# A product-key expert lookup: forming and searching 136 of each head's 256 pair sums

## What is computed

```python
sim = jnp.einsum('pbnhd,hkpd->pbnhk', queries, keys)
v0, i0 = jax.lax.top_k(sim[0], TOPK)
all_scores = v0[..., :, None] + i0[..., None, :].astype(v0.dtype)
all_scores = all_scores.reshape(*all_scores.shape[:-2], -1)
scores, pk_indices = jax.lax.top_k(all_scores, TOPK)
h = jax.nn.gelu(jnp.einsum('bnd,bnhkd->bnhk', q, jnp.take(weight_down_embed, pk_indices, axis=0)))
h = h * jax.nn.softmax(scores, axis=-1)
out = jnp.einsum('bnhk,bnhkd->bnd', h, jnp.take(weight_up_embed, pk_indices, axis=0))
```

## Time and profile before

| | us |
|---|---|
| median of 3 runs | 2607.98 |
| lowest and highest run | 2607.81, 2615.81 |
| the profiled execution | 2608.87 |
| its span, first to last instruction | 2607.1 |

### The profile page before, as it was taken

How to read it: one execution, slowest core, us unless ns; L and a number is a source line. 1 busy time by engine, 2 the same in 40 slices (tenths; PEclk the granted TensorE clock), 3 DMA queues, 4 the chain that set the end, 5 groups by cost and what they waited for, 6 DMA issues and landing times.

```text
span 2607.1 us, 30788 instructions
## 1 busy us (share of the span) xinstructions
PE 2241.5 (86%) x11214; PEld 1274.1 (49%) x11214; DVE 1378.6 (53%) x4080; ACT 725.1 (28%) x1573; POOL 813.7 (31%) x532
## 2 busy tenths in 40 slices
PE   1999984998967999988899999988999989888863
PEld 0455552443323444446654567668666633444431
DVE  5455676778965666651142443420222232599996
ACT  3111121221004444432211365552111110244442
POOL 2028888887875556640000000000000000022221
PEclk9998776997988999999999989998999989989977
DMA  9982222222227666642000020003000050000000
GB/s 358 419 322 3 3 3 19 4 4 19 3 35 203 162 169 174 170 119 110 1 11 38 9 98 1 1 1 131 1 1 1 1 133 0 1 4 9 8 8 12
DMA packets 90264, 180.59 MB, mean 69 GB/s; under 512 B 65109, under 2 KB 66070, under 8 KB 74135
## 3 DMA queue, kind: packets, MB, share of 16 engines
q1 hardware_dynamic: 44367, 176.77, 20.9%
q0 software_dynamic: 45072, 1.46, 5.1%
q10 hardware_dynamic: 674, 0.39, 0.1%
HBM read 110.27 MB, written 68.31 MB: 68 GB/s over the span
## 4 chain that ended last, share of the span: by engine, by line
PE 45%; POOL 19%; DVE 14%; issue 7%; DMA 5%; SPq 5%; ACT 4%; DVEq 0%; ACTq 0%; POOLq 0%
POOL edge_table L503 16%; PE banks L189 10%; PE banks L1999 6%; PE banks L2026 5%; DMA edge_table<-arena 5%; SPq L293 5%; PE banks L1432 3%; PE banks L1255 3%; PE banks L1268 2%; PE banks L1810 2%; PE banks L1837 2%; PE banks L1824 2%; POOL arena L1212 2%; PE banks L1859 2%; DVE arena L1180 1%
## 5 line engine op out<-in xcount | busy, mean ns | idle before, releaser
L189 PE MATMUL banks<-arena 128*125 128x512 f32 (+1 forms) x1280 | 601.7, 619 | 84.3 <-ACT arena L2503 75.0
L503 POOL DMA_INDIRECT edge_table<-arena x313 | 490.8, 1568 | 248.1 <-DMA edge_table<-arena 157.7
L189 PEld LDWEIGHTS banks<-arena 128*125 128x125 f32 x1280 | 245.2, 200 | 374.6 <-issue 278.8
L1180 DVE TENSOR_TENSOR arena<-banks,arena 125x500 f32<-125x500 f32 x200 | 208.4, 1051 | 148.9 <-ACT banks L1232 146.5
L1212 POOL TENSOR_TENSOR arena<-arena 125x500 f32<-125x500 f32 x180 | 222.8, 1248 | 147.0 <-DVE arena L1180 141.5
L1255 PE MATMUL banks<-arena 64*125 64x250 f32 x800 | 141.3, 430 | 50.9 <-DVE arena L1180 44.4
L2337 POOL MEMSET arena<- 128x1024 f32 x2 | 1.8, 952 | 579.8 <-DVEq L140 579.8
L1947 DVE SCALAR_TENSOR_TENSOR arena<-banks,arena 125x512 f32<-125x512 f32 x80 | 60.1, 751 | 203.7 <-PE banks L2026 203.7
L1232 ACT ACTIVATE banks<-banks 125x500 f32<-125x500 f32 x200 | 114.5, 573 | 169.7 <-PE banks L1258 169.3
L183 PE MATMUL banks<-arena 125*128 125x125 f32 x560 | 94.8, 309 | 69.5 <-DVE arena L177 50.0
L1999 PEld LDWEIGHTS banks<-arena 128*128 128x128 f32 x1280 | 144.2, 192 | 6.9 <-issue 6.8
(11 more groups left out here) (318 smaller groups left out, 3598.7 us busy)
## 6 DMA issues: line engine op xcount, KB each, us to landing
edge_table<-arena SPq DMA_DIRECT2D x24, 2250.0 KB, 36.1
arena<-edge_table SPq DMA_DIRECT2D x50, 984.4 KB
arena<-L_ffn_W SPq DMA_DIRECT2D x4, 2048.0 KB, 8.2
arena<-edge_table SPq DMA_DIRECT2D x50, 114.3 KB
adjacency<-arena SPq DMA_DIRECT2D x50, 109.4 KB
arena<-adjacency SPq DMA_DIRECT2D x10, 546.9 KB
edge_table<-arena POOLq DMA_INDIRECT x313, 3.0
arena<-x SPq DMA_DIRECT2D x1, 2240.0 KB
```

What stands on the lines that cost most here:

```text
L189: last = nc.tensor.matmul(dst, xT[:, i, :], w[:, i, 0:n], start=(i == 0), stop=(i == k - 1))
L503: pool.indirect_dma_start(d["table"], bass.IndirectOffsetOnAxis(ap=cell[0:EP, c:c + 1].bitcast(U32), axis=0), vals[0:EP, c * ROW:(c + 1) * ...
L1180: nc.vector.tensor_tensor(P_g[n % PRING][0:TP, :].rearrange("p (e n) -> p e n", e=2), two_scores(n), ring[(c * TILES + b) % RING][0:TP, :, ...
```

## The change

A head's table is no longer formed whole. The values `v0` come sorted, so row a of the table belongs to the a-th largest value. The first 8 rows are formed with all 16 columns, 128 cells; of the other 8 rows only the cell in the column with the largest key index is formed, 8 cells. A cell in one of these rows and another column is beaten by at least 16 others, so the 16 largest are among the 136. (`PAIR_CELLS` is 136, `LOW` 128.)

- VectorE, after the cast: the largest index of each head (`fmax_p`, a reduction), and at the start of `pairs` a comparison of each index with it, which gives 1 in its column and 0 elsewhere (`largest_p`).
- GpSimd: two additions in place of one (8 x 128 and 8 x 8 cells), the second after the reduction; the product of `S` and `M` over 1088 cells; and a new product `U` that spreads the 8 cells of each head back over their 128 places by the comparison. `U` has one buffer and waits for TensorE's sums of the tile before.
- VectorE's four search groups and ScalarE's two groups run over 136 columns of a head in place of 256. Their counts stay.
- TensorE sums the heads in two groups: 8 products of 128 columns from `S` into the first half of the bank, and 8 of 128 columns from `U` into the second.

```diff
@@ -2337,19 +2342,33 @@
                 last = nc.gpsimd.memset(w, 0.0)
             last.then_inc(s_zeroed, 1)
             for t in range(TILES):
-                pool.wait_ge(p_f, t + 1)
+                pool.wait_ge(p_f, 3 * t + 1)
                 if t >= 2:
                     pool.wait_ge(p_ws, t - 1)
                 S, M = S_p[t % 2][0:TP, :], M_p[t % 2][0:TP, :]
+                by_cell = S.rearrange("p (h n) -> p h n", h=HEADS)
+                v0 = v0_p[t % 2][0:TP, :].rearrange("p (h a) -> p h a", a=TOPK)
+                f0 = f0_p[t % 2][0:TP, :].rearrange("p (h b) -> p h b", b=TOPK)
+                fmax = fmax_p[t % 2][0:TP, :].unsqueeze(2)
+                is_max = largest_p[t % 2][0:TP, :].rearrange("p (h b) -> p h b", b=TOPK)
                 nc.gpsimd.tensor_tensor(
-                    S.rearrange("p (h a b) -> p h a b", h=HEADS, a=TOPK),
-                    v0_p[t % 2][0:TP, :].rearrange("p (h a) -> p h a", a=TOPK).unsqueeze(3)
-                    .to_broadcast([TP, HEADS, TOPK, TOPK]),
-                    f0_p[t % 2][0:TP, :].rearrange("p (h b) -> p h b", b=TOPK).unsqueeze(2)
-                    .to_broadcast([TP, HEADS, TOPK, TOPK]), ALU.add).then_inc(p_sp, 1)
+                    by_cell[:, :, 0:LOW].rearrange("p h (a b) -> p h a b", a=TOP_ROWS),
+                    v0[:, :, 0:TOP_ROWS].unsqueeze(3).to_broadcast([TP, HEADS, TOP_ROWS, TOPK]),
+                    f0.unsqueeze(2).to_broadcast([TP, HEADS, TOP_ROWS, TOPK]), ALU.add).then_inc(p_sp, 1)
+                pool.wait_ge(p_f, 3 * t + 2)
+                nc.gpsimd.tensor_tensor(by_cell[:, :, LOW:PAIR_CELLS], v0[:, :, TOP_ROWS:TOPK],
+                                        fmax.to_broadcast([TP, HEADS, TOPK - TOP_ROWS]), ALU.add).then_inc(p_sp, 1)
 
                 pool.wait_ge(p_e, 2 * t + 2)
                 nc.gpsimd.tensor_tensor(S, S, M, ALU.mult).then_inc(p_w, 1)
+                pool.wait_ge(p_w, 2 * t + 1)
+                pool.wait_ge(p_f, 3 * t + 3)
+                if t >= 1:
+                    pool.wait_ge(p_ws, t)
+                nc.gpsimd.tensor_tensor(
+                    U_p[0:TP, :].rearrange("p (h a b) -> p h a b", h=HEADS, b=TOPK),
+                    by_cell[:, :, LOW:PAIR_CELLS].unsqueeze(3).to_broadcast([TP, HEADS, TOPK - TOP_ROWS, TOPK]),
+                    is_max.unsqueeze(2).to_broadcast([TP, HEADS, TOPK - TOP_ROWS, TOPK]), ALU.mult).then_inc(p_w, 1)
...
                 nc.vector.tensor_copy(f0_p[t % 2][0:TP, :], i0_p[t % 2][0:TP, :].bitcast(U32)).then_inc(p_f, 1)
+                dve.wait_ge(p_f, 3 * t + 1)
+                nc.vector.tensor_reduce(fmax_p[t % 2][0:TP, :], by_head(f0_p[t % 2], TOPK), AX_X, ALU.max).then_inc(p_f, 1)
 
             def pairs(t):
 
                 S, M, top = S_p[t % 2], M_p[t % 2], top_p[t % 2]
-                dve.wait_ge(p_sp, t + 1)
+                dve.wait_ge(p_f, 3 * t + 2)
+                nc.vector.tensor_tensor(by_head(largest_p[t % 2], TOPK), by_head(f0_p[t % 2], TOPK),
+                                        fmax_p[t % 2][0:TP, :].unsqueeze(2).to_broadcast([TP, HEADS, TOPK]),
+                                        ALU.is_equal).then_inc(p_f, 1)
+                dve.wait_ge(p_sp, 2 * t + 2)
...
@@ -2571,12 +2599,17 @@
 
             def weights(t):
 
-                pe.wait_ge(p_w, t + 1)
+                pe.wait_ge(p_w, 2 * t + 1)
                 if t >= 1:
                     pe.wait_ge(p_x, t)
                 for h in range(HEADS):
-                    last = nc.tensor.matmul(bank(3)[0:TP, 0:KEYS], ident[0:TP, 0:TP],
-                                            S_p[t % 2][0:TP, KEYS * h:KEYS * (h + 1)],
+                    nc.tensor.matmul(bank(3)[0:TP, 0:LOW], ident[0:TP, 0:TP],
+                                     S_p[t % 2][0:TP, PAIR_CELLS * h:PAIR_CELLS * h + LOW],
+                                     start=(h == 0), stop=(h == HEADS - 1))
+                pe.wait_ge(p_w, 2 * t + 2)
+                for h in range(HEADS):
+                    last = nc.tensor.matmul(bank(3)[0:TP, LOW:KEYS], ident[0:TP, 0:TP],
+                                            U_p[0:TP, (KEYS - LOW) * h:(KEYS - LOW) * (h + 1)],
                                             start=(h == 0), stop=(h == HEADS - 1))
                 last.then_inc(p_ws, 1)
```

25 lines of the change are left out of this document (16 added, 9 removed).

## The result

The changed kernel takes 2565.48 us (median; 2562.40 to 2571.48), the kernel before 2609.51 beside it (2607.81 to 2615.81). The ratio is 0.982, 95% interval 0.9804 to 0.9836. The forecast was 2556 in a range of 2546 to 2570: the time is in the range and 9.5 us above the forecast. The profiled execution took 2563.54 us, with a span of 2561.7.

A forecast was written before the change was run, and what follows sets the result against it. VectorE's own work plus one wait per tile for GpSimd's pair sums bounds the kernel. Savings of 40.7 + 9.8 + 1.3 = 51.8 us gave 2557.1 for a profile and 2556 us for the median, range 2546 to 2570.

The forecast's parts named there:

- Searches: VectorE's 32 searches a tile, first search to first exponential: 256 to 136 columns, 12.66 to 8.59 us; ten tiles 40.7 us.
- Pair sums: From the cast's start to the first search: 4.00 to 3.07 us in tiles 2 to 7; 9.8 us in all.
- ScalarE and GpSimd hidden: ScalarE's exponentials and relus end 1.6 us earlier; GpSimd's products stay hidden by 6 us before the next pair sums.
- The comparison: VectorE's added instruction before the first search: +0.2 us, able to meet GpSimd's addition in tiles 8 and 9 only.
- TensorE: Its loop per tile takes 27.4 us against a 28.6 us period: hidden by 1.2 us, output projection near 2.0 us.
- The tail and the clock: After tile 9's first exponential starts: ScalarE 1.6 us earlier, the split sum costs 0.3; 1.3 us gained.
- The sum against a median: 51.8 us off a profiled 2608.87 us, 0.9 above the median: 2557.1 for a profile, 2556 for the median.
- (a): TensorE becomes the bound, its clock staying lower from output projection through queries: loop 30.9 us, time 2568; chance 0.08.
- (b): VectorE's searches do not shorten with length: only 11 us gained, time 2597; chance 0.05.
- (c): VectorE's searches shorten in full proportion to length: time 2542; chance 0.04.
- (d): GpSimd's two additions end over 8.0 us after the cast's start, making the kernel slower; at 9 us, 2621; chance 0.03.
- (e): The change does not do what it says, only possible by a longer search of another kind; given no chance of its own.

The follow-up runs named there:

- the searches alone: Kernel before with all 256 sums formed but VectorE's four search groups run over 136 columns of a head: 2576.55 us, ratio 0.9848.
- the comparison elsewhere: Changed kernel with the comparison taken off VectorE, GpSimd subtracting the largest index and ScalarE making the mark: 2566.73 us, ratio 0.9806.
- The sums alone: Kernel before with the new pair sums, reduction and comparison, but searches, exponentials, relus and product still over 256 columns: 2605.61 us, ratio 0.9963.
- the first trace: First profile of the changed kernel against the kernel before: 2565.48 us, ratio 0.9820, last stage 297.6 us.
- the second: Changed kernel profiled once more, nothing altered: 2570.36 us, ratio 0.9825 to the kernel before, last stage 301.1 us.
- the repeated half: Changed kernel with the second half of TensorE's head sum formed twice (2567.15 us, ratio 0.9818) or three times (2585.04 us, ratio 0.9884).
- four lengths: Kernel before searching 200 or 72 columns (2595.93 and 2551.02 us, one run each), beside 136 and 256; a search took 0.353, 0.220, 0.286, 0.412 us.

## Why the prediction was right, and where it was off

- **Searches** (40.7 us): right. The row taken for the slope, L2452 against L2435 in the earlier trace rows, gave 0.285 and 0.15 + 1.06 ns a column; the search itself has 0.286 and 0.145 + 1.04. That it came so near was in part luck: the two rows differ in more than length, since L2452 reads one input from a bank and L2435 does not, and neither is a search. M to P was forecast at 8.59 and is 8.64; the searches alone took 40.2 us off the stage.
- **Pair sums** (9.8 us): right. The first addition takes 1.92 us (1.93 forecast), the second 0.30 (0.2). VectorE's own work ends at C + 3.06 (3.07), and with the comparison elsewhere GpSimd's sums release VectorE at C + 2.51 (2.5). The sums alone gave 9.9. By the Trainium skill's figure for two inputs (GPSIMD Engine Reference, § 3.1) the estimate for the addition was 2.2 us, and the stage would have gained 1 less; the measurement, 1.92, decides against it here.
- **ScalarE and GpSimd hidden**: right. The eight exponentials take 2.48 us and the relus 3.22 to 3.24, against 3.28 and 4.04 in the earlier trace rows; GpSimd's two products, 2.48 and 1.91, end long before its next addition, which comes after 6.05 us of idle.
- **The comparison** was priced at 0.2 us with the remark that it may meet the addition in tiles 8 and 9. It does, and takes 1.3 there. The price did not reach the time, because VectorE would have waited for the sums anyway: the prediction had some 1.2 us of idle before the first maximum there, and the row shows 0.19, the rest hidden in the longer comparison.
- **TensorE** (hidden, 27.4 us a loop, slack 1.2): right in kind. The projection fell to 1.98 us in turns 1 to 6, and doubling a half of the sum measured the loop as 26.73 and the slack as 1.95. The 0.7 too much: the transposes behind the projection rose to the higher clock as well (four records of L186 take 0.59 us where they take 1.02 in a slow turn), and the split cost next to nothing (3.73 us for both halves, 3.69 before in the earlier trace rows, where 3.95 was taken).
- **The tail and the clock** (1.3 us): this step failed. The prediction asked of each idle stretch only whether the output projection behind it would be slow. In the changed kernel other work has idle ahead of it too: the sums in turns with 2 to 8 us of idle, and those of the tail. The trace of before had such a row, the one of 5.63 us above, and the prediction did not use it. In the first trace this cost 0.8 us in the third tile, 0.3 in the ninth and nothing in the tail, whose gain was 1.6; in the second it cost 0.7, 0.2 and, in the last tile, 1.6, and the tail was 0.6 us longer than before. The stage's gain was 50.5 and 46.9 us against 51.8.
- **The sum against a median**: the stages ahead of the last were taken as fixed at the profiled execution's, 2259.07. That was the earliest start of all fourteen traces. A start at 2264.15 and a stage of 297.6 give the span of 2561.7. The forecast 2556 missed by 9.5: 5.1 from where the stage began, 1.3 in that trace's stage, and the rest because its execution (2563.54) was itself 1.9 under the median, where the one before had been taken as 0.9 over it; the three make 9.2, and rounding the rest. The ratios, 0.982 and 0.9825, stand for 46 to 47 us of about 2610, close to the smaller of the two gains of the stage, 46.9.
- **Rivals.** (a) is refuted by the repeated half; (b), no shortening, and (c), in proportion, by 0.286 us and by the line through four lengths; (d), additions ending after C + 8.0, by sums ready at C + 2.5; (e) did not arise.
